# Last masked tiles cut by targets, a halved last store, an earlier load and a new order of steps in a graph attention kernel

## The reference, cut to what matters

```python
h = relu(layernorm(x))
out = relu(h @ mlp1_w + mlp1_b)                     # 128 -> 256
out = elu(gat(out, None, W_fc, a_fc)) + out         # layer 1, no mask
out = relu(out @ mlp2_w + mlp2_b)                   # 256 -> 128
x = x + relu(elu(gat(out, adj, W_hand, a_hand)) + out)   # layer 2, masked
h = relu(layernorm(x))
return x + gat(h, adj, W, a)                        # layer 3, masked
# gat(v): h = v @ W; e = leaky_relu(h@a1 [:, None] + h@a2 [None, :]); mask;
#         elu(softmax(e) @ h)
```

## Time and profile before

| | |
|---|---|
| median of three executions | 432.27 us |
| profiled execution | 432.44 us |
| its span, first to last instruction | 430.6 us |
| PE (matmul) busy | 411.8 us, 96% |
| DVE busy | 358.1 us, 83% |
| ACT busy | 314.4 us, 73% |
| POOL busy | 25.0 us, 6% |
| TensorE clock granted, mean | 0.996 |

### The profile page before, as it was taken

The page is one execution under the profiler, slowest core; times in us unless marked ns, Lnnn a source line. Parts: engine busy times, 40 slices in busy tenths (PEclk is TensorE's granted clock), DMA queues, the critical chain, the costliest instruction groups (busy, mean ns, idle before and its releaser), DMA issues.

```text
span 430.6 us, 8695 instructions
## 1 busy us (share of the span) xinstructions
PE 411.8 (96%) x2545; PEld 353.0 (82%) x2545; DVE 358.1 (83%) x1222; ACT 314.4 (73%) x760; POOL 25.0 (6%) x53
## 2 busy tenths in 40 slices
PE   6899999999999999999999999999999999989782
PEld 4688788887888989797998788989889799869772
DVE  6788589968888898889898787987798989889973
ACT  2545867778876978686777878479678887799873
POOL 0000000000001000000100010100100110010000
PEclk9999999999999999999999999999999999999998
DMA  7745145142332123232321422223120223101101
GB/s 216 247 150 172 30 115 143 48 112 73 100 122 75 51 99 98 52 100 74 121 76 51 123 57 94 66 63 95 51 74 2 73 77 99 47 4 32 43 2 54
DMA packets 39445, 36.41 MB, mean 85 GB/s; under 512 B 4064, under 2 KB 30304, under 8 KB 39392
## 3 DMA queue, kind: packets, MB, share of 16 engines
q1 hardware_dynamic: 37392, 33.17, 25.8%
q10 hardware_dynamic: 2000, 2.63, 1.9%
HBM read 31.46 MB, written 4.32 MB: 83 GB/s over the span
## 4 chain that ended last, share of the span: by engine, by line
issue 66%; PE 20%; DVE 6%; POOL 5%; ACT 2%; POOLq 0%; DVEq 0%; ACTq 0%
PE bank L1403 6%; POOL fmax L713 5%; PE bank L1392 4%; PE bank L1493 3%; PE bank L1382 2%; DVE prob L1177 2%; PE bank L1421 1%; DVE u L1231 1%; PE bank L1443 1%; PE bank L1432 1%; DVE stats L1010 1%; PE bank L1411 1%; PE bank L1322 0%; ACT e L885 0%; PE bank L1372 0%
## 5 line engine op out<-in xcount | busy, mean ns | idle before, releaser
L1493 PEld LDWEIGHTS bank<-ext,prob 128*128 128x128 f32 x1024 | 119.6, 192 | 5.5 <-issue 3.1
L1493 PE MATMUL bank<-ext,prob 128*128 128x129 f32 x1024 | 122.6, 276 | 0.6 <-DVE prob L1177 0.3
L1403 PE MATMUL bank<-ext,prob 128*128 128x257 f32 x512 | 118.4, 380 | 0.0
L1403 PEld LDWEIGHTS bank<-ext,prob 128*128 128x128 f32 x512 | 95.0, 190 | 16.7 <-issue 4.2
L1177 DVE SCALAR_TENSOR_TENSOR prob<-prob,square,mask_t 128x512 f32<-128x512 f32 x102 | 73.5, 741 | 5.1 <-ACT prob L833 5.0
L1392 PE MATMUL bank<-wfc_sb,o_t 128*128 128x259 f32 x256 | 63.3, 382 | 0.0
L833 ACT ACTIVATE prob<-row,square 128x512 f32<-128x512 f32 x78 | 54.5, 721 | 0.7 <-DMA row<-row_scratch 0.6
L1392 PEld LDWEIGHTS bank<-wfc_sb,o_t 128*128 128x128 f32 x256 | 46.4, 191 | 9.2 <-issue 3.5
L1231 DVE SCALAR_TENSOR_TENSOR u<-e,y 128x512 f32<-128x512 f32 (+1 forms) x70 | 44.6, 639 | 9.5 <-issue 4.7
L877 ACT ACTIVATE y<-bank,recip 128x128 f32<-128x128 f32 x128 | 39.1, 366 | 16.5 <-DVE recip L1223 16.4
L885 ACT ACTIVATE e<-y,minus_one 128x512 f32<-128x512 f32 (+1 forms) x70 | 47.8, 686 | 1.1
(11 more groups left out here) (96 smaller groups left out, 496.6 us busy)
## 6 DMA issues: line engine op xcount, KB each, us to landing
row<-row_scratch SPq DMA_DIRECT2D x36, 256.0 KB, 3.3
moments_row<-moments_scratch SPq DMA_DIRECT2D x13, 512.0 KB, 3.9
x_in<-in_x SPq DMA_DIRECT2D x16, 256.0 KB, 4.7
x_res<-in_x SPq DMA_DIRECT2D x16, 256.0 KB, 4.2
out<-y_out SPq DMA_DIRECT2D x16, 256.0 KB, 3.7
normed<-in_x_t SPq DMA_DIRECT2D x14, 256.0 KB, 4.3
row_scratch<-square_t SPq DMA_DIRECT2D x144, 0.5 KB
adj_sb<-in_adj ACTq DMA_DIRECT2D x1, 1024.0 KB, 6.6
```

The source lines that it names most:

```text
L1403: last = nc.tensor.matmul(filled[:, 0:H + 1], gat1.targets(b, t, c), gat1.features_and_one(b, t), start=(t == 0), stop=(t == C - 1))
L1493: last = nc.tensor.matmul(filled[:, e * (D + 3):e * (D + 3) + D + 1], L.targets(b, t, c), L.features_and_one(b, t), start=(t == 0), stop=( ...
```

## The change

1. **The cut.** A new table `CUT = {1: (), 2: (15,)}` names layer 3 of batch 15. There the four steps `prob3_0.15` to `prob3_3.15` no longer make one source tile with 512 targets each. Each makes two source tiles with 256 targets: steps 0 and 1 the first half of the targets for tiles 0, 1 and 2, 3, steps 2 and 3 the second half. TensorE's step q of that attention waits for steps 2q+1 and 2q+2 only.
2. **The store.** The result of batch 15 is stored in two transfers of two tiles, each after its own half of `result`; the first counts on a semaphore of its own, on which SyncE waits at the end.
3. **The loads.** SyncE's list begins `load.0 load.1 load_t.0` in place of `load.0 load_t.0 load.1`; the residual loads of the first batches (`load_again.0`, `load_again.1`) and `load.4`, `load_t.3` come earlier, the rest of the weights later.
4. **The order.** All five lists are permuted; no step is added or taken out. The idle transposes ahead of `roots.0` go from 3 to 2.

```diff
+CUT = {1: (), 2: (15,)}
-STIRRED = {("roots", 0): 3, ("mlp1_0", 0): 3, ...
+STIRRED = {("roots", 0): 2, ("mlp1_0", 0): 3, ...

 "sync":
-        load.0 load_t.0 load.1 weights load.2 load.3 weights_rest load.4 load_t.3 load.5 load.6 load_t.4 row0.3
+        load.0 load.1 load_t.0 weights load.2 load_again.0 load.3 load.4 load_t.3 weights_rest load.5 load.6
+        row0.3 load.7 row0.4 load_t.4 load.8 load_again.1 load_t.5 load_t.6 row0.5 load.9 row0.6 row1.3
 "scalar":
-        weights root1.0 root1.1 mlp1_0.0 mlp1_1.0 turn1.1 root1.2 adjacency mlp1_0.1 h1_0.0 mlp1_1.1 h1_1.0
+        weights root1.0 root1.1 mlp1_0.0 mlp1_1.0 turn1.1 adjacency root1.2 mlp1_0.1 h1_0.0 mlp1_1.1 turn1.2
 "vector":
-        constants stats1.0 norm1.0 vectors ones normt.0 stats1.1 scores1 norm1.1 stats1.2 norm1.2 stats1.3
-        norm1.3 stats1.4 max1.0 args1.0 edgeless prob1_0.0 prob1_1.0 max1.1 prob1_2.0 masks_0 scores23
+        constants ones stats1.0 norm1.0 vectors stats1.1 normt.0 scores1 norm1.1 stats1.2 norm1.2 stats1.3
+        stats1.4 max1.0 norm1.3 args1.0 edgeless prob1_0.0 prob1_1.0 prob1_2.0 max1.1 prob1_3.0 args1.1
...
-        att1_3.15 elu1_0.15 prob3_0.12 elu1_1.15 max2.14 prob3_1.12 args2.14 z_0.15 z_1.15 root2n.13
+        att1_3.15 prob3_0.12 elu1_0.15 elu1_1.15 root2n.13 max2.14 z_0.15 args2.14 z_1.15 prob3_1.12
...
-        prob3_0.15 prob3_1.15 prob3_2.15 prob3_3.15 guard att3_1.14 elu3_0.14 att3_0.15 elu3_1.14
-        result_0.14 att3_1.15 result_1.14 elu3_0.15 result_0.15 elu3_1.15 result_1.15 flag
+        prob3_0.15 prob3_1.15 att3_1.14 prob3_2.15 prob3_3.15 guard att3_0.15 elu3_0.14 result_0.14
+        elu3_1.14 att3_1.15 result_1.14 elu3_0.15 flag result_0.15 elu3_1.15 result_1.15
 "tensor":
-        ... h1_3.1 scores23 empties h1_0.2 att1_0.0 att1_1.0
+        ... row1.0 h1_3.1 mlp1_1.2 att1_0.0 empties row1.1 h1_0.2 h1_1.2 att1_1.0
...
-        turn2.13 h2_0.14 h2_1.14 z_0.15 z_1.15 h3_0.13 h3_1.13 row2.14 mlp2.15
+        h2_0.14 h2_1.14 turn2.13 z_0.15 h3_0.13 z_1.15 h3_1.13 row2.14 mlp2.15
...
             def store(b):
+                rest = slice(0, C)
+                if not general and b.n == B - 1:
+                    sp.wait_ge(*y_ready.at(b, 1))
+                    sp.dma_start(out_v[b.n][:, 0:C // 2], y_out[:, b.slot, 0:C // 2]).then_inc(s_half_stored, 16)
+                    rest = slice(C // 2, C)
                 sp.wait_ge(*y_ready.at(b, 2))
-                sp.dma_start(out_v[b.n], y_out[:, b.slot]).then_inc(stored.sem(b), 16)
+                sp.dma_start(out_v[b.n][:, rest], y_out[:, b.slot, rest]).then_inc(stored.sem(b), 16)

+        def cut_parts(t):
+            return (2 * (t % 2), 2 * (t % 2) + 1), slice(t // 2 * (N // 2), (t // 2 + 1) * (N // 2))

 (scale_row)
+                if cut(b, L):
+                    tiles, half = cut_parts(t)
+                    for k in tiles:
+                        last = nc.scalar.activation(L.prob_of(b)[:, k, half], row_of(b, L)[:, half], ACT.Copy,
+                                                    scale=L.buv[:, b.slot, 2, k:k + 1])
+                    last.then_inc((s.scaled_first if t == 0 else s.scaled_row).sem, 1)
+                    return
 (prob_scaled)
+                if cut(b, L):
+                    tiles, half = cut_parts(t)
+                    for k in tiles:
+                        p = L.prob_of(b)[:, k, half]
+                        last = nc.vector.scalar_tensor_tensor(out=p, in0=p, scalar=L.buv[:, b.slot, 1, k:k + 1],
+                                                              in1=mask_t[:, k, half], op0=ALU.max, op1=ALU.min)
+                    last.then_inc(s.prob_ready.sem, 1)
+                    return
 (attend_masked)
-                        if c == 0 and factored(L, general):
+                        if not general and cut(b, L):
+                            if e == 0 and t % 2 == 0:
+                                pe.wait_ge(*s.prob_ready.at(b, 2 * q + t // 2 + 1))
+                        elif c == 0 and factored(L, general):
                             pe.wait_ge(*s.prob_ready.at(b, t + 1))
```

More of the change, by code:

```diff
@@ L69 @@
[L69 to L72, removed]
-        att1_2.4 prob3_2.0 mlp2.3 args2.2 prob3_3.0 att1_3.4 elu1_1.4 h2_0.3 h2_1.3 h3_0.1 h3_1.1 mlp1_0.6
@@ new lines @@
+        h1_0.8 att1_2.6 att1_3.6 elu2.4 elu1_1.6 prob3_3.2 h1_1.8 turn2.3 h1_2.8 root2.3 att2_0.5 h3_0.3
+        att2_1.5 att3_0.2 h3_1.3 h1_3.8 att3_1.2 elu3.2 args3.3 elu2.5 mlp2.6 root2.4 mlp1_0.9 att1_0.7 args1.8
+        mlp1_1.9 att1_1.7 turn2.4 prob3_1.3 h2_0.6 prob3_2.3 prob3_3.3 h2_1.6 h3_0.4 h3_1.4 root1.14 att1_2.7
+        elu1_0.7 h1_0.9 att3_0.3 att1_3.7 att3_1.3 args2.6 elu3.3 h1_1.9 args3.4 elu1_1.7 h1_2.9 h1_3.9
+        att1_0.8 att1_1.8 turn2.5 mlp1_0.10 root2.5 mlp1_1.10 mlp2.7 prob2_1.6 args1.9 root1.15 prob2_2.6
@@ new lines @@
+        prob2_3.10 args3.8 elu2.9 att1_0.11 att1_1.11 h1_0.13 att1_2.11 elu1_0.11 h1_1.13 att1_3.11 root2.9
+        elu1_1.11 h1_2.13 att2_0.10 turn2.9 att2_1.10 h1_3.13 args1.13 prob3_1.8 elu2.10 h3_0.9 h3_1.9
+        att1_0.12 prob3_2.8 att1_1.12 prob3_3.8 args3.9 mlp2.11 att1_2.12 h2_0.11 elu1_0.12 att1_3.12 h2_1.11
+        att3_0.8 elu1_1.12 att3_1.8 elu3.8 args2.11 prob3_1.9 mlp1_0.14 att1_0.13 mlp1_1.14 prob3_2.9 prob3_3.9
+        att1_1.13 elu1_0.13 att1_2.13 mlp2.12 prob2_1.11 att3_0.9 turn2.10 att1_3.13 root2.10 prob2_2.11
@@ new lines @@
+        masks_3 elu1_0.0 att1_3.0 prob1_3.1 att1_0.1 elu1_1.0 normt.3 att1_1.1 z_0.0 norm1.5 max1.2 z_1.0
+        args1.2 normt.4 att1_2.1 scores23 att1_3.1 norm1.6 elu1_0.1 stats1.7 elu1_1.1 prob1_0.2 prob1_1.2
+        max2.0 max1.3 prob1_2.2 args2.0 z_0.1 prob1_3.2 z_1.1 att1_0.2 stats1.8 args1.3 prob2_0.0 norm1.7
+        row1.3 prob2_1.0 normt.5 prob2_2.0 stats1.9 att1_1.2 max2.1 att1_2.2 args2.1 norm1.8 prob2_3.0
+        prob2_0.1 prob2_1.1 att2_0.0 prob1_0.3 elu1_0.2 prob1_1.3 prob1_2.3 att1_3.2 att2_1.0 prob1_3.3
@@ L211 @@
-        turn_o2.15 h3_0.14 h3_1.14 row3.14 turn2.15 h3_0.15 h3_1.15 att3_0.14 row3.15 att3_1.14 att3_0.15
-        att3_1.15
+        warm means.0 roots.0 scores1 mlp1_0.0 mlp1_1.0 turn1.1 h1_0.0 mlp1_0.1 mlp1_1.1 h1_1.0 turn1.2 h1_2.0
+        h1_3.0 h1_0.1 mlp1_0.2 h1_1.1 h1_2.1 row1.0 h1_3.1 mlp1_1.2 att1_0.0 empties row1.1 h1_0.2 h1_1.2
+        att1_1.0 att1_2.0 att1_3.0 h1_2.2 att1_0.1 h1_3.2 scores23 z_0.0 att1_1.1 mlp1_0.3 z_1.0 att1_2.1
+        mlp1_1.3 mlp2.0 att1_3.1 h2_0.0 h1_0.3 h1_1.3 row1.2 h2_1.0 h1_2.3 h1_3.3 z_0.1 mlp1_0.4 z_1.1 att1_0.2
```

287 lines of the change are left out of this document (141 added, 146 removed).

## The result

| | before | after |
|---|---|---|
| median of 20 executions each, side by side | 432.58 us | 431.69 us |
| lowest and highest | 432.09, 434.21 | 430.77, 433.24 |
| profiled execution | 432.44 us | 430.77 us |
| its span | 430.6 us | 429.0 us |

The ratio of the medians is 0.9975, with a 95% interval of 0.9964 to 0.9986: faster by 0.9 us in 432, which is less than the 0.5% that I had called distinguishable. The profiled executions differ by 1.67 us. The 20 of before have a median 0.31 us above the 432.27 of its first three executions, on which the forecast was built.

A forecast was written before the change was run, and what follows sets the result against it. TensorE was taken to bound the kernel from 20 to 380 us. Terms -0.3 - 0.3 - 0.6 - 0.45 = -1.65 took the profiled 432.44 to 430.8, and the median, 0.17 lower, to 430.7 us; range 429.2 to 433.2.

The forecast's parts named there:

- The load and the start: First 20 us: batch 1's earlier load lets its statistics precede normt.0, first h1 at 12.25 for 12.56; -0.3 us.
- Around 380: Around 380 us: the 1.67 us wait stays, the 0.31 us wait before mlp2 of batch 15 goes; -0.3 us.
- Rival B: 380 to 402.97 us: VectorE's bound stretch shortens too, half its 2.3 us idle going; 429.5 us; 22%.
- The cut: Batch 15's last tiles: TensorE ends 1.0 us earlier, ScalarE's line then bounds, store issued at 424.95; -0.6 us.
- Rival A: Batch 15's last tiles: small operations cost full duration, ScalarE's tiles end 1.5 us later; 431.8 us; 13%.
- The halved store: Last store: half of 0.9 us of transfer is saved, the first half being issued earlier; -0.45 us.
- Those 2.7 us stay: End of program: the 2.7 us from the last store's landing to the span's end do not change.
- Between 20 and 380: 20 to 380 us: all other moves priced at 0, nothing idle to win; bounds 0 and +2 us.
- Rival D: 20 to 380 us: the new order opens waits about the size of what is won; 432.3 us; 13%.
- The adjacency: Before the first attention: edgeless starts about 19.8, costing nothing until 20.8; 0 taken from 0 to 1.2 us.
- rival C: Before the first attention: the adjacency lands late and TensorE idles; a start at 23.3 gives 433.2 us; 10%.

The follow-up runs named there:

- e5: Kernel before with only x of batch 1 loaded second, ahead of batch 0's x by features: 432.80 us, ratio 1.0006.
- e6: Kernel before with the swapped loads and, on VectorE, ones ahead of stats1.0 and stats1.1 ahead of normt.0: 433.72 us, ratio 1.0007.
- e1: Changed kernel with batch 15's last masked tiles made whole again; order, loads and halved store kept: 432.11 us, ratio 0.9991.
- e4: Kernel before, in its own order, with only batch 15's last masked tiles cut: 432.24 us, ratio 0.9994.
- e3: Kernel before with only the store of batch 15 in halves: 432.98 us, ratio 1.0006.
- e7: Changed kernel with batch 1's statistics back behind normt.0 on VectorE, loads as changed: 432.90 us, ratio 0.9995.
- e8: Changed kernel with one whole last store and the first layer's weights second in SyncE's load list: 433.23 us, ratio 0.9999.
- e2: Changed kernel with batch 15 stored in one transfer: 431.55 us, ratio 0.9978.
- e9: Changed kernel with three idle transposes ahead of batch 0's roots for two: 432.69 us, ratio 0.9985.
- e12: Changed kernel with ScalarE issuing the adjacency transfers ahead of batch 0's first MLP activations: 432.11 us, ratio 0.9983.

## Why the prediction was right, and where it was not

The time of 430.7 us was forecast for a median that came out at 431.69, inside the range. The median moved by 0.9 us, a little over half of the forecast 1.6. That the sum of -1.65 meets the profiled difference of -1.67 is luck: the term of the halved store did not come, a gain between 20 and 380 us that the sum has at 0 did, and the profile of after is the lowest of its 20 times.

- **The load and the start, -0.3:** right in mechanism and size. The statistics came at the forecast 6.7, mlp1 at 9.31 for a forecast 9.6, h1 at 12.16 for 12.25. The load alone is worth nothing (e5), with VectorE's order 0.40 (e6, one profile against one).
- **Around 380, -0.3:** the wait of 0.31 went and the 1.67 stayed. 0.16 of it arrived (0.96 to 1.12; from z to mlp2 it takes 2.58 us for 2.74). The rest went into another short wait, in the step ahead of mlp2: `row2.14` needs `square` from ScalarE, which is done at 382.89 (382.68 + 0.21), and its first matmul starts at 383.04, about 0.28 us after it was due, too little for a bracket in the row. Rival B, a shorter VectorE stretch, did not come: from mlp2 of batch 15 to its scaled tiles it is 31.95 us for 31.93.
- **The cut, -0.6:** right; -0.68 against before, 0.75 in e1. ScalarE's pitch is 3.03 / 8 = 0.38 with the tail, the 0.37 I took, and its last copies wait for nothing, as forecast. VectorE's is 1.65 / 4 = 0.41 with its tail, 0.40 from start to start, and not the 0.34 I took from two unlike operations in a row: four more operations cost it 0.5 us where I had nothing (3.26 us for eight in e4, for 2.74), and the reciprocal at 417.92 stands between them now. Its last tile is there 4.20 us after ScalarE's first for a forecast 3.90, and TensorE ends 6.00 after it for a forecast 5.65 (6.68 before): of its gain 0.68 arrived and not 1.0. The last copies start at 421.69, when ScalarE's line is through; the reciprocal behind TensorE's end is there at the same time, so two bounds meet, and the size came out right with one of two pitches off. Rival A's condition, ScalarE over 0.42 apart, was not met. On the rule that I set aside, the Trainium skill, "VectorE: DVE Perf Modes", section on the TRN2 errata (a fixed latency for each operation, so tiles of 512 and more), the trace of after is on its side: 0.40 us from start to start for 256 columns against 0.67 for 512 leaves 0.13 fixed (twice 0.40 less 0.67), about twice what I had estimated from the page's 58 cycles. The cut pays all the same, because TensorE starts on it sooner.
- **The halved store, -0.45:** this step failed. I took the 2.7 us behind the landing as a constant, "Those 2.7 us stay", as if the end waited for the landing. In the order of before it waits for TensorE's branch, so the landing's 0.5 us (e3) moves nothing. In the new order it does wait for the landing, 1.6 us behind it, and the half is worth 0.4 to 0.5 us (e7 against e8 and e2). But in that order, whose move of `flag` I gave no term, the last store also lands after 3.5 us where I had 1.85. Net, the end comes 5.2 us after the issue for 5.1 before.
- **Between 20 and 380, 0:** wrong by 0.56 us, and outside my bounds of 0 and +2. I read 359.99 busy of 360.00 as a stretch in which nothing can be won. It holds short waits that the count does not show, and the new order has about 0.5 us less of them. Rival D does not appear.
- **The adjacency, 0:** 0.15 us of waiting in the profile of after and next to nothing lost; rival C's mechanism is real. VectorE reached the reduction where I put it, near 19.8, but the microsecond of cover behind it is not there: a start at 20.83, where I had no cost, costs 0.7 us (e9). Rival C needed more than twice that to turn the sign.
- **From the profile to the median:** the step that I did not have. I carried the profiled execution's 1.7 us over to the median, which moved 0.9. The lower eleven of 20 executions of before have a median of 432.31 and those of after one of 431.29; the upper nine 433.75 and 432.73. Both groups moved by 1.0. The second kernel's groups stand close (431.76, then 431.97), so this line between them is drawn by count; with it, late starts are not what ate the rest. The profile of after is the lowest of its 20, 0.52 under the median of its lower group; that of before is 0.13 over its own. These two make the 0.65 us between 1.67 and 1.02. The adjacency is one thing that spreads the new lower group, over 430.8 to 431.8: the order of before reached that reduction at about 21.4, the new one at 19.9, inside the spread of its landing. That this is all of the spread is argued, not shown.

## To carry over

A stretch in which the profile counts an engine as 100% busy can still hold short waits: compare the time between two common points, and the distances from start to start, not the idle time. A smaller last store shortens the program only if the landing is what its end waits for, so look for what each engine does behind its last step, the branch on a flag too, before counting on it. When a step is pulled forward to use up slack against a transfer, count with the spread of that transfer's landing over executions, and read several profiles before carrying a difference of one over to the median.

## What was not expected of the hardware

- In the first microseconds the same matmuls come at either of two durations, and TensorE's continuous work up to then does not tell which: after and e7 have nearly the same rows until 6.65 us, then eight matmuls take 0.95 us in one and 1.71 in the other. It goes on until about 13 us and costs 1.8 us. The granted-clock column shows it in e2 (0.50 after a wait of 0.78 us) and not in e7.
- The transfer of 1 MB (the adjacency) landed 6.2 to 9.0 us after its issue over thirteen profiles, and 5.6 after it when it was issued 3.3 us earlier (e12).
- TensorE's branch at the end of the program takes 3.7 to 4.4 us, that of every other engine under 0.1. It ends the program in five profiles.
- The same store of 128 KB lands after 1.8 us in e3 and after 3.5 to 4.0 in seven profiles whose flag is written earlier; of 256 KB after 2.3 or 2.4 us and after 4.2 or 4.3.
